# Fused attention and expert kernel: fewer, larger GpSimd operations between result scatters, and two small reorderings around the attention transposes

## The chip, the cores and the metric

The kernel runs on 1 core of one Trainium2 chip (trn2). The metric is the device time of one execution in microseconds (us). PE is TensorE, DVE is VectorE, ACT is ScalarE, POOL is GpSimd, and SP is the engine whose queue issues the plain DMAs. The kernel before takes 235.84 us, the median of three runs (235.73 to 238.3).

## The reference, cut to what matters

```python
x = L0_attn_x                                   # (4, 1024, 128) float32
xn = layernorm(x)
q, k = xn @ w_q, xn @ w_k                       # 64 columns each
attn = softmax(where(causal, q @ k.T * 64 ** -0.5, -inf))
attention = attn @ (xn @ w_v1 @ w_v2)
logits = xn @ w_router.T                        # 16 experts, top 1
s = sigmoid(logits) * one_hot(argmax(logits), 16)
gate, up = split((s * xn) @ gate_up_proj)       # 256 columns each, of the chosen expert
expert = (up * silu(gate)) @ down_proj
shared = silu(xn @ w_gate.T) * (xn @ w_up.T) @ w_down.T
out = x + attention + shared + expert
```

All of it is float32. The kernel splits each float32 operand of most products into a high and a low part and uses three products.

## The kernel before, in words

The 4096 tokens are 32 tiles of 128. They form 4 batches b = 0 to 3 of 8 tiles, each of two halves ("groups") of 4 tiles. Each engine has its own program, written out by hand; engines meet only at counting semaphores. An instruction waits at the head of its engine's queue until a semaphore has reached a value, and all behind it on that engine wait with it. Nothing is reordered by a planner. The program has these parts, with the times of the profiled execution:

- **Up to about 64 us**: layer norm, projections, router and shared expert. The router gives each token a slot in a table sorted by expert (48 tiles of 128 slots, 24 pairs of tiles).
- **Routing scatter, 59.6 to 111.9 us, on POOL (L454 to L459)**: 32 indirect DMAs write the token rows to their slots in DRAM (`scratch`), with a small weight subtraction (`weights_lo`, L428) after each. Beside it PE, ACT and DVE do the **attention of batches 0, 1 and half of 2** (`phase_c`).
- **Expert part, 114.8 to 203 us** (`phase_d`): for each of the pairs p = 0 to 23, SP loads 256 sorted rows (`xe`, two buffers), PE transposes them (`transpose_rows`), and three steps of PE, ACT and DVE make the result `y` (three buffers). POOL then scatters it to its tokens with two indirect DMAs (L505), 47 in all since the last pair has one tile.
- **The end, 203 to 233 us** (`phase_e`): attention of the other half of batch 2 and of batch 3 on PE, ACT and DVE. SP loads `y` back in 8 groups, POOL adds it to the residual (L513), and SP stores the result.

Around the change the names are these. In the expert part POOL runs a loop over the scatters t = 0 to 46 (pair p = t // 2). Ahead of each scatter it does small work: `keep_ids` (L461) copies the token numbers of pair p + 4 out of the `xe` buffer, `keep_scores` (L467) its scores, and `last_keys_hi` and `last_keys_lo` (L477, L480) split the keys of batch 3 in pieces of `K_PIECE` = 24 columns, 43 pieces of each kind for 1024 columns. The two key copies use only POOL's otherwise unneeded time; their result is first used by `scores` of batch 3 (L1237). SP issues the load of pair n + 2 into the buffer of pair n once PE has transposed pair n (`xet_done`) and POOL has kept both its ids and its scores (L354 to L357). POOL starts a pair's scatters once ACT has copied its result (`y_ready`, L494). PE's step p does gate and up of pair p, down of pair p - 2, the transposes of the hidden rows of pair p - 1 and the row transposes of pair p + 2 (L1370 to L1381); the registers that name the experts are loaded every second step (L1336).

In the attention, `scores(b, i)` computes the scores of tile i of batch b, DVE takes the row maximum (`row_max`), ACT the exponentials (`exp`, L1004, one per tile, counted in `exp_done`), PE transposes them block by block (`transposes(b, n)`, L1254), ACT copies the block (`keep_pt`) and PE multiplies it with the values (`weigh`). A block of `transposes` takes up to four tiles of one half and waits for the exponentials of all four before its first.

Of the kernel before, what the change touches and what calls it, by code (L numbers as in the profile page):

```python
# [30 lines left out]
GT = 4  # L31
# [6 lines left out]
def build(nc, x, w_small, w_gate_up, w_down, scratch, y_rows, out):  # L38
    B, S, EMB = x.shape
    NT = B * S // P  # L40
    NG = NT // GT
    BT = S // P
# [5 lines left out]
    NP = NS // 2  # L48
# [15 lines left out]
    with ExitStack() as ctx:  # L64
# [8 lines left out]
        def sb(name, shape, dt=F32):  # L73
            t = nc.alloc_sbuf_tensor_at(name, shape, dt, offset=top[0])
            top[0] += size(shape, dt)
            return t
# [55 lines left out]
        k_raw = sb("k_raw", [P, S])  # L132
        k_hi, k_lo = sb("k_hi", [P, S], F32R), sb("k_lo", [P, S], F32R)
# [39 lines left out]
        def sem(name, n=None):  # L173
            if n is None:
                return ctx.enter_context(nc.semaphore(name))
            return [ctx.enter_context(nc.semaphore(f"{name}{i}")) for i in range(n)]
# [27 lines left out]
        k_hi_ready, k_lo_ready, k_hi_pieces = sem("k_hi_ready"), sem("k_lo_ready"), sem("k_hi_pieces")  # L204
        s_done, max_ready, exp_done = sem("s_done"), sem("max_ready"), sem("exp_done")
# [29 lines left out]
        def flat(ap):  # L235
            return ap.rearrange("p a b -> p (a b)")
# [43 lines left out]
        def used(p):  # L280

            return 1 if isinstance(p, int) and p == NP - 1 else 2
# [94 lines left out]
        def _(pool):  # L377
# [83 lines left out]
            def keep_ids(p):  # L461

                q = p % 2
                pool.wait_ge(xe_loaded[q], 8 * (p - q) + 16)
                pool.tensor_copy(ids[:, 2 * p:2 * p + 2], xe[q][:, :, ID].bitcast(U32)).then_inc(ids_kept, 1)
# [5 lines left out]
                    pool.wait_ge(eh_ready, p - NY + 1)  # L471
                pool.tensor_copy(slot_score[:, p % NY, :], xe[q][:, :, SCORE]).then_inc(scores_kept, 1)

            def k_piece(n):
                return slice(n * K_PIECE, min((n + 1) * K_PIECE, S))

            def last_keys_hi(n):  # L477
                pool.tensor_copy(k_hi[:, k_piece(n)], k_raw[:, k_piece(n)]).then_inc(k_hi_pieces, 1)

            def last_keys_lo(n):  # L480
                cols = k_piece(n)
                pool.wait_ge(k_hi_pieces, n + 1)
                last = pool.tensor_tensor(k_lo[:, cols], k_raw[:, cols], k_hi[:, cols].bitcast(F32), ALU.subtract)
                if cols.start < S // 2 <= cols.stop or cols.stop == S:
                    last.then_inc(k_lo_ready, 1)
# [6 lines left out]
            for p in range(NP):  # L492
                pool.wait_ge(ids_kept, p + 1)
                pool.wait_ge(y_ready, p + 1)  # L494
                for t in range(2 * p, 2 * p + used(p)):
                    if t and p + AHEAD - 1 + t % 2 < NP:
                        if t % 2:
                            keep_scores(p + AHEAD)
                        else:
                            keep_ids(p + AHEAD - 1)  # L500
                    if t and (t - 1) * K_PIECE < S:
                        last_keys_hi(t - 1)
                    if t > 1 and (t - 2) * K_PIECE < S:
                        last_keys_lo(t - 2)
                    pool.indirect_dma_start(y_rows, bass.IndirectOffsetOnAxis(ap=ids[:, t:t + 1], axis=0),  # L505
                                            y[p % NY][:, t % 2, :], None, bounds_check=NT * P - 1,
                                            oob_is_err=False).then_inc(y_sent[p % NY], 16)

            for g in RETURN_ORDER:
                t = slice(g * GT, (g + 1) * GT)  # L510
# [6 lines left out]
        def _(dve):  # L517
# [62 lines left out]
            def add_shared(g):  # L580
                b, u = g // 2, g % 2
                dve.wait_ge(ffn_done, FIRST + g + 1)
                r = flat(res[:, bass.ds(g * GT, GT), :])
                dve.tensor_tensor(r, acc[u][:, :], r, ALU.add).then_inc(shared_added[u], 1)
# [222 lines left out]
            def first_half(b, first):  # L807
                if first:
                    for i in range(BT - 2):
                        row_max(b, i)  # L810
                        if i == 1:
                            add_shared(NG - 3)
                        if i == 4:
                            add_shared(NG - 2)
                            add_shared(NG - 1)
                row_max(b, BT - 2)
                row_max(b, BT - 1)
                if not first:
                    add_attention(b - 1, 1)
                if b == 1:  # L820
                    name_experts()
# [277 lines left out]
        def _(pe):  # L1099
# [154 lines left out]
            def transposes(b, n):  # L1254
                kb, c0 = block_of(n)
                g = 0 if n < GT else 1
                pe.wait_ge(exp_done, FIRST + b * BT + (g + 1) * GT)
                pe.wait_ge(pt_ready, FIRST + b * STEPS + max(n - 1, 0))
                if b == B - 2 and n == GT:
                    pe.wait_ge(xel_ready, NP)  # L1260
                if b == B - 2 and n == GT + 1:
                    pe.wait_ge(eht_ready, NP)
                for r in range(c0 // P, GT):
                    last = pe.transpose(mid[n % 2][:, r * P:(r + 1) * P],  # L1264
                                        prob[g * GT + r][:, kb * P:(kb + 1) * P], identf[:, :])
                last.then_inc(pt_done, 1)
# [20 lines left out]
            def first_half(b, first):  # L1287
                if first:
                    down(NG - 2)
                    for i in range(GT + 1):  # L1290
                        scores(b, i)
                    down(NG - 1)
                    pe.wait_ge(ranks_used, 1)
                    transposes(b, 0)
                else:
                    transposes(b, 0)
                    scores(b, BT - 1)
                if first:
                    scores(b, GT + 1)
                for n in range(GT):  # L1300
                    if first and n < 2:
                        scores(b, GT + n + 2)
                    if first and n == GT - 1:
                        weigh(b, n)
                        transposes(b, n + 1)
                        continue
                    if b == B - 2 and n == GT - 2:
                        pe.wait_ge(exp_done, FIRST + b * BT + BT - 1)
                        transpose_rows(0, 0)
                    if not (b == B - 2 and n == GT - 1):  # L1310
                        transposes(b, n + 1)
                    weigh(b, n)
                    if b == B - 2 and n == GT - 2:
                        pe.wait_ge(pt_ready, FIRST + b * STEPS + n + 1)
                        transpose_rows(1, 1)
# [89 lines left out]
CODE = 4  # L1405
NY = 3
AHEAD = 4
K_PIECE = 24
RETURN_ORDER = (0, 1, 2, 3, 4, 6, 7, 5)
FLY = 4  # L1410
FIRST = 1
# [36 lines left out]
```

## Time and profile before

| | |
|---|---|
| median of 3 runs | 235.84 us |
| profiled execution, its own time | 234.89 us |
| its span | 233.2 us |
| PE busy | 212.0 us, 91% |
| POOL busy | 158.1 us, 68% |
| POOL from the first result scatter to the end of the last | 127.69 to 207.21 us |
| TensorE clock granted | full throughout (1.00) |

The times in a profile line count from the start of the span. A timeline line has the start, the duration, the engine, the line of the kernel, the operation with the tensors it writes and reads, and how often it is repeated back to back; a bracket at the end tells how long the engine was idle before it and what released it ("issue" is a wait for nothing that the profile can name). Small operations on one engine overlap a little, so the distance from start to start is what counts.

### The profile page before, as it was taken

To read this page: it belongs to the slowest core of one execution; us is meant where nothing else is said; L and a number is where in the kernel's file an instruction comes from. 1 tells how busy PE (TensorE), PEld (TensorE's weight loads), DVE (VectorE), ACT (ScalarE), POOL (GpSimd) and SP (SyncE) were. 2 spreads that over 40 slices of the span, in tenths; PEclk is the share of its full clock that TensorE was granted. 3 is DMA by queue.
4 is the path that set the end of the run, shared out by engine and by line. 5 is a ranking of instruction groups with operands and counts; after the bars stand their busy time and mean duration, and the time that the engine had idled before them with its cause. 6 is when DMAs were issued, how large, how long until landed. Compare 5 with 4: busy or idle time off the path is not lost.

```text
span 233.2 us, 5014 instructions
## 1 busy us (share of the span) xinstructions
PE 212.0 (91%) x1415; PEld 182.3 (78%) x1417; DVE 146.2 (63%) x352; ACT 128.6 (55%) x305; POOL 158.1 (68%) x308
## 2 busy tenths in 40 slices
PE   4999999999997699899989999799989998899994
PEld 4978888897785598698767887677767786788794
DVE  3889679788764579879846657365456545304512
ACT  2377777877374556666764543344334424645741
POOL 3475956900788888888111989788988989845910
PEclk9999999999999999999999999999999999999999
DMA  6999999970181117215521122222231220009931
GB/s 132 337 381 300 274 208 200 155 291 3 40 210 45 35 49 179 82 37 135 133 67 42 56 80 54 80 70 65 79 87 52 77 78 10 0 6 285 297 90 46
DMA packets 30021, 28.27 MB, mean 121 GB/s; under 512 B 2579, under 2 KB 27162, under 8 KB 29360
## 3 DMA queue, kind: packets, MB, share of 16 engines
q1 hardware_dynamic: 27472, 23.77, 40.6%
q0 software_dynamic: 2528, 4.24, 5.9%
q8 instruction: 11, 0.18, 0.3%
q14 instruction: 10, 0.08, 0.1%
HBM read 14.28 MB, written 10.50 MB: 106 GB/s over the span
## 4 chain that ended last, share of the span: by engine, by line
PE 57%; POOL 21%; issue 8%; DMA 6%; DVE 3%; ACT 1%; SPq 1%; POOLq 0%; ACTq 0%
POOL scratch L457 14%; PE big L1103 7%; PE acc L1365 7%; PE big L1104 6%; PE big L1105 6%; POOL wel L431 5%; DMA xe<-scratch 5%; PE acc L1283 4%; PE acc L1163 4%; PE mid L1354 3%; PE mid L1264 3%; PE mid L1230 3%; PE mid L1113 2%; PE big L1283 2%; PE mid L1133 2%
## 5 line engine op out<-in xcount | busy, mean ns | idle before, releaser
L505 POOL DMA_INDIRECT y_rows<-y,ids x47 | 47.0, 1000 | 13.1 <-issue 8.2
L457 POOL DMA_INDIRECT scratch<-rows,slot x32 | 33.7, 1054 | 17.8 <-DVE slot L729 12.7
L1283 PE MATMUL acc<-vr_all,pt 128*128 128x128 f32 x246 | 35.9, 280 | 2.8 <-ACT pt L1016 2.1
L859 DVE COPY eht<-mid 128x512 f32<-128x512 f32 (+1 forms) x24 | 16.3, 681 | 33.5 <-PE mid L1354 22.9
L1283 PEld LDWEIGHTS acc<-vr_all,pt 128*128 128x128 f32 x246 | 31.6, 191 | 4.9 <-ACT pt L1016 2.3
L779 DVE TENSOR_REDUCE negmax<-big 128x1 f32<-128x128 f32 (+7 forms) x32 | 23.9, 754 | 18.1 <-PE big L1251 17.5
L1075 ACT COPY y<-acc 128x256 f32<-128x256 f32 (+1 forms) x24 | 8.8, 368 | 43.9 <-PE acc L1365 39.0
L1016 ACT COPY pt<-mid 128x512 f32<-128x512 f32 (+3 forms) x48 | 22.8, 475 | 17.0 <-PE mid L1264 14.9
L1004 ACT ACTIVATE prob<-big,negmax 128x128 f32<-128x128 f32 (+7 forms) x32 | 23.8, 743 | 14.1 <-DVE negmax L779 8.8
L1365 PEld LDWEIGHTS acc<-wed,eht 128*128 128x128 f32 x188 | 24.4, 191 | 3.8 <-issue 2.1
L1365 PE MATMUL acc<-wed,eht 128*128 x188 | 25.1, 276 | 1.3 <-DVE eht L859 1.3
L1103 PE MATMUL big<-weh,xeh 128*128 x47 | 20.7, 440 | 4.4 <-issue 3.8
L1264 PE MATMUL mid<-identf,prob 128*128 128x128 f32 x144 | 23.6, 274 | 0.7 <-ACT prob L1004 0.7
L865 DVE SCALAR_TENSOR_TENSOR eh<-esg,slot_score,big 128x256 f32<-128x256 f32 x47 | 20.5, 478 | 1.8 <-ACT esg L1082 1.3
L1082 ACT ACTIVATE esg<-big,slot_score 128x256 f32<-128x256 f32 x47 | 19.9, 478 | 1.2 <-PE big L1105 1.2
L1248 PE MATMUL big<-k_hi,q_hl 128*128 128x512 f32 (+3 forms) x48 | 18.6, 388 | 1.9 <-ACT prob L1004 1.6
L1251 PE MATMUL big<-k_lo,q_hl 128*128 128x512 f32 (+3 forms) x48 | 18.6, 393 | 0.0
L441 POOL TENSOR_SCALAR rows<-res,ln,ln 128x128 f32<-128x128 f32 x20 | 18.2, 918 | 0.5
L1105 PE MATMUL big<-weh,xel 128*128 x47 | 18.5, 393 | 0.0
L1104 PE MATMUL big<-wel,xeh 128*128 x47 | 18.4, 392 | 0.0
L1264 PEld LDWEIGHTS mid<-identf,prob 128*128 128x128 f32 x144 | 17.3, 142 | 1.4 <-ACT prob L1004 1.1
L393 POOL TENSOR_TENSOR ln<-ln,minus_half 128x4 f32<-128x4 f32 x8 | 8.9, 1115 | 10.1 <-DVE ln L557 10.1
(141 smaller groups left out, 473.5 us busy)
## 6 DMA issues: line engine op xcount, KB each, us to landing
we_raw<-w_gate_up SPq DMA_DIRECT2D x4, 1024.0 KB, 10.4
scratch<-blank SPq DMA_DIRECT2D x1, 3120.0 KB, 27.8
xe<-scratch SPq DMA_DIRECT2D x24, 130.0 KB
q_raw<-qk_all SPq DMA_DIRECT2D x8, 256.0 KB
k_raw<-qk_all SPq DMA_DIRECT2D x8, 256.0 KB
wed<-w_down SPq DMA_DIRECT2D x1, 2048.0 KB, 32.0
expert_out<-y_rows SPq DMA_DIRECT2D x8, 256.0 KB, 4.7
out<-res SPq DMA_DIRECT2D x7, 256.0 KB, 3.7
```

The costliest lines, as they stand in the source:

```text
L457: pool.indirect_dma_start(scratch, bass.IndirectOffsetOnAxis(ap=slot[:, t:t + 1], axis=0), rows[:, t, :], None).then_inc(row_sent[t % FLY] ...
L505: pool.indirect_dma_start(y_rows, bass.IndirectOffsetOnAxis(ap=ids[:, t:t + 1], axis=0), y[p % NY][:, t % 2, :], None, bounds_check=NT * P ...
L779: dve.tensor_reduce(negmax[:, i:i + 1], buf[:, at:at + (i + 1) * P], AX.X, ALU.max, negate=True).then_inc(max_ready, 1)
L865: last = dve.scalar_tensor_tensor(out=eh[q][:, v, :], in0=esg[q][:, v, :], scalar=slot_score[:, m, v:v + 1], in1=big[q][:, v * GC + FE:(v ...
L1004: act.activation(prob[i][:, 0:(i + 1) * P], buf[:, at:at + (i + 1) * P], ACT.Exp, bias=negmax[:, i:i + 1], accum_out=den[:, i:i + 1]).then ...
L1016: act.copy(pt[n % 2][:, c0:GC], mid[n % 2][:, c0:GC]).then_inc(pt_ready, 1)
L1103: pe.matmul(dst, wh, mh, start=True, stop=False)
L1104: pe.matmul(dst, wh, ml, start=False, stop=False)
L1105: return pe.matmul(dst, wl, mh, start=False, stop=True)
L1264: last = pe.transpose(mid[n % 2][:, r * P:(r + 1) * P], prob[g * GT + r][:, kb * P:(kb + 1) * P], identf[:, :])
L1283: last = pe.matmul(weighed(b, g, r), pt[n % 2][:, cols], v, start=kb == 0 and (r == 0 or own_bank), stop=True, skip_group_check=True)
L1365: last = pe.matmul(acc[q][:, v * P:(v + 1) * P], eht[q][:, v, c, :], flat(wed[:, bass.ds(e[v], 1), c * P:(c + 1) * P]), start=c == 0, stop ...
```

## The change

- The low parts of batch 3's keys are made in pieces of 48 columns, one per pair, in place of 24 columns ahead of each scatter. The high parts stay at 24 columns. `last_keys_lo` waits for the two high pieces that it covers.
- `keep_ids` moves from the even scatter of the next pair to the odd scatter, right behind `keep_scores`.
- In batch 0, `scores(0, 5)` comes ahead of the first block of transposes.
- `transposes` waits for the exponentials of each tile just before that tile's transpose, in place of all four before the first.
- DVE adds the shared expert's last group one row maximum later.

```diff
+            def last_keys_hi(half):
+                cols = slice(half * K_PIECE // 2, min((half + 1) * K_PIECE // 2, S))
+                if cols.start < S:
+                    pool.tensor_copy(k_hi[:, cols], k_raw[:, cols]).then_inc(k_hi_pieces, 1)
             def last_keys_lo(n):
-                pool.wait_ge(k_hi_pieces, n + 1)
+                cols = slice(n * K_PIECE, min((n + 1) * K_PIECE, S))
+                pool.wait_ge(k_hi_pieces, min(2 * n + 2, -(-2 * S // K_PIECE)))
...
                 for t in range(2 * p, 2 * p + used(p)):
-                    if t and p + AHEAD - 1 + t % 2 < NP:
-                        if t % 2:
+                    if t % 2:
+                        if p + AHEAD < NP:
                             keep_scores(p + AHEAD)
-                        else:
-                            keep_ids(p + AHEAD - 1)
-                    if t and (t - 1) * K_PIECE < S:
-                        last_keys_hi(t - 1)
-                    if t > 1 and (t - 2) * K_PIECE < S:
-                        last_keys_lo(t - 2)
+                            keep_ids(p + AHEAD)
+                        last_keys_hi(2 * p)
+                    elif p:
+                        last_keys_hi(2 * p - 1)
+                        if 1 < p and (p - 2) * K_PIECE < S:
+                            last_keys_lo(p - 2)
...
-                        if i == 4:
+                        if i == GT:
                             add_shared(NG - 2)
+                        if i == GT + 1:
                             add_shared(NG - 1)
...
-                pe.wait_ge(exp_done, FIRST + b * BT + (g + 1) * GT)
                 pe.wait_ge(pt_ready, FIRST + b * STEPS + max(n - 1, 0))
...
                 for r in range(c0 // P, GT):
+                    pe.wait_ge(exp_done, FIRST + b * BT + g * GT + r + 1)
...
                     pe.wait_ge(ranks_used, 1)
-                    transposes(b, 0)
-                else:
-                    transposes(b, 0)
+                    scores(b, GT + 1)
+                transposes(b, 0)
+                if not first:
                     scores(b, BT - 1)
-                if first:
-                    scores(b, GT + 1)
...
-K_PIECE = 24
+K_PIECE = 48
```

On POOL, in the expert part, two pairs of scatters before:

```order
L465 COPY ids<-xe_92 128x2
L478 CAST k_hi<-k_raw 128x24
L483 TENSOR_TENSOR k_lo<-k_raw,k_hi 128x24
L505 DMA y_rows<-y_145,ids 4096x128
L472 COPY slot_score<-xe_95 128x2
L478 CAST k_hi<-k_raw 128x24
L483 TENSOR_TENSOR k_lo<-k_raw,k_hi 128x24
L505 DMA y_rows<-y_145,ids 4096x128
```

and the same place in the changed kernel:

```order
L477 CAST k_hi<-k_raw 128x24
L482 TENSOR_TENSOR k_lo<-k_raw,k_hi 128x48
L504 DMA y_rows<-y_146,ids 4096x128
L472 COPY slot_score<-xe_92 128x2
L465 COPY ids<-xe_92 128x2
L477 CAST k_hi<-k_raw 128x24
L504 DMA y_rows<-y_146,ids 4096x128
```

Ahead of the even scatter there was an ids copy, a high and a low piece and ahead of the odd one a scores copy and the same; now the even one has a high and a wider low piece, and the odd one has both copies and a high piece. That is five operations per pair in place of six.

On PE, after the down product of the last group in batch 0 (`prob_123` to `prob_127` are the exponentials of tiles 0 to 3), before:

```order
L1264 MATMUL mid<-identf,prob_123 128x128 [waits pt_ready,exp_done,ranks_used]
L1264 MATMUL mid<-identf,prob_124 128x128
L1264 MATMUL mid<-identf,prob_125 128x128
L1264 MATMUL mid<-identf,prob_127 128x128
L1248 MATMUL big<-k_hi,q_hl 128x512 [waits exp_done]
L1251 MATMUL big<-k_lo,q_hl 128x512
```

and now:

```order
L1248 MATMUL big<-k_hi,q_hl 128x512 [waits exp_done,ranks_used]
L1251 MATMUL big<-k_lo,q_hl 128x512
L1248 MATMUL big<-k_hi,q_hl 128x256
L1250 MATMUL big<-causal,identb 128x128
L1251 MATMUL big<-k_lo,q_hl 128x256
L1264 MATMUL mid<-identf,prob_123 128x128 [waits exp_done,pt_ready]
L1264 MATMUL mid<-identf,prob_124 128x128 [waits exp_done]
L1264 MATMUL mid<-identf,prob_125 128x128 [waits exp_done]
L1264 MATMUL mid<-identf,prob_127 128x128 [waits exp_done]
```

The scores of tile 5 stand ahead of the block, and each transpose of a block carries a wait of its own. The second of these holds for all 48 blocks of the kernel (144 transposes, 96 waits more).

## Rows read from the trace of the kernel before

**Rows 1.** The page, part 2: busy tenths in 40 slices of 5.83 us.
```profile
PE   4999999999997699899989999799989998899994
...
POOL 3475956900788888888111989788988989845910
```
**Rows 2.** POOL's timeline: a full round from one scatter (t = 3) to the next.
```profile
132.60 1.00 POOL L505 DMA_INDIRECT y_rows<-y,ids  x1 [0.17 <-issue]
133.61 0.20 POOL L465 COPY ids<-xe 128x2 uint32<-128x2 uint32 x1
133.74 0.21 POOL L478 CAST k_hi<-k_raw 128x24 fp32r<-128x24 f32 x1
133.90 0.24 POOL L483 TENSOR_TENSOR k_lo<-k_raw,k_hi 128x24 fp32r<-128x24 f32 x1
134.31 1.01 POOL L505 DMA_INDIRECT y_rows<-y,ids  x1 [0.17 <-issue]
```
**Rows 3.** PE's timeline: starts of steps 3 and 4, last row transposes (end of step 21).
```profile
126.81 0.47 PE L1103 MATMUL big<-weh,xeh 128*128 x1
...
129.74 0.47 PE L1103 MATMUL big<-weh,xeh 128*128 x1
...
192.65 0.43 PE L1230 MATMUL mid<-identf,xe 128*128 128x128 f32 x2
```
**Rows 4.** Waits on PE, 119 to 203 us: us in total, times, longest.
```profile
PE big L1103 <- issue: 3.8, 9, 0.9
PE mid L1230 <- DMA xe<-scratch: 2.4, 4, 1.6
```
**Rows 5.** Waits of SP's queue over the whole span, same columns.
```profile
SPq L356 <- POOL ids L465: 25.9, 9, 3.2
```
**Rows 6.** POOL's timeline: places where it was late, and the last ids before a load.
```profile
142.14 0.48 POOL L472 COPY slot_score<-xe 128x2 f32<-128x2 f32 x1
...
151.73 0.18 POOL L465 COPY ids<-xe 128x2 uint32<-128x2 uint32 x1 [0.78 <-issue]
...
176.15 0.18 POOL L465 COPY ids<-xe 128x2 uint32<-128x2 uint32 x1 [0.43 <-issue]
...
188.18 0.20 POOL L472 COPY slot_score<-xe 128x2 f32<-128x2 f32 x1
...
189.91 0.18 POOL L465 COPY ids<-xe 128x2 uint32<-128x2 uint32 x1
```
**Rows 7.** ACT's timeline: the copy of pair 7's result.
```profile
151.23 0.37 ACT L1075 COPY y<-acc 128x256 f32<-128x256 f32 x1 [2.12 <-PE acc L1365]
```
**Rows 8.** Chain of waits: start, duration, what.
```profile
110.30 4.38 DMA scratch<-rows,slot
...
144.55 3.66 DMA xe<-scratch
```
**Rows 9.** Line L431: shortest/median/longest in ns, 64 columns each.
```profile
L431 POOL TENSOR_TENSOR wel<-we_raw,weh x32: 325/330/761, 61.3 to 111.6; 128x64 fp32r<-128x64 f32 x32
```
**Rows 10.** PE's timeline: first transposes of batch 3's second half.
```profile
220.64 0.66 PE L1264 MATMUL mid<-identf,prob 128*128 128x128 f32 x4 [0.34 <-ACT prob L1004]
```
**Rows 11.** Timelines of POOL (sums 2 to 6) and DVE (batch 3, first half).
```profile
213.59 6.22 POOL L513 TENSOR_TENSOR res<-res,expert_out 128x512 f32<-128x512 f32 x5 [0.77 <-DMA expert_out<-y_rows]
...
221.65 1.13 DVE L799 SCALAR_TENSOR_TENSOR res<-acc,rden,res 128x128 f32<-128x128 f32 x4 [0.83 <-PE acc L1283]
```
**Rows 12.** Timelines of POOL and DVE at the same moment of the routing scatter.
```profile
79.70 0.76 POOL L431 TENSOR_TENSOR wel<-we_raw,weh 128x64 fp32r<-128x64 f32 x1
...
79.59 0.69 DVE L701 TENSOR_TENSOR k_lo<-k_raw,k_hi 128x512 fp32r<-128x512 f32 x1
```
**Rows 13.** Line L1124, one wait per transpose: columns as in rows 9.
```profile
L1124 PE MATMUL acc<-identf,rows x32: 270/272/332, 9.0 to 47.7; 128*128 128x128 f32 x32
```
**Rows 14.** The page, part 5: attention transposes (count, busy us, mean ns).
```profile
L1264 PE MATMUL mid<-identf,prob 128*128 128x128 f32 x144 | 23.6, 274 | 0.7 <-ACT prob L1004 0.7
L1264 PEld LDWEIGHTS mid<-identf,prob 128*128 128x128 f32 x144 | 17.3, 142 | 1.4 <-ACT prob L1004 1.1
```

More of the change, by code:

```diff
@@ L472, in keep_scores @@
                 pool.tensor_copy(slot_score[:, p % NY, :], xe[q][:, :, SCORE]).then_inc(scores_kept, 1)
[L474 to L478, printed above, removed]
+            def last_keys_hi(half):
+                cols = slice(half * K_PIECE // 2, min((half + 1) * K_PIECE // 2, S))
+                if cols.start < S:
+                    pool.tensor_copy(k_hi[:, cols], k_raw[:, cols]).then_inc(k_hi_pieces, 1)
             def last_keys_lo(n):
-                cols = k_piece(n)
-                pool.wait_ge(k_hi_pieces, n + 1)
+                cols = slice(n * K_PIECE, min((n + 1) * K_PIECE, S))
+                pool.wait_ge(k_hi_pieces, min(2 * n + 2, -(-2 * S // K_PIECE)))
                 last = pool.tensor_tensor(k_lo[:, cols], k_raw[:, cols], k_hi[:, cols].bitcast(F32), ALU.subtract)
```

## The prediction

> **What bounds the kernel now.** I read the busy slices of the page first: PE and POOL are both nearly full from 115 to 207 us [rows 1], so the page alone doesn't tell which of them sets the pace of the expert part. POOL's timeline does. From one scatter to the next it takes 134.31 - 132.60 = 1.71 us [rows 2], 1.705 on average over such rounds, with no gap but the 0.17 us ahead of each scatter; a pair is two rounds, 3.41 us. PE's steps 3 and 4 start 129.74 - 126.81 = 2.93 us apart when their rows are there [rows 3]. But from the start of step 4 to the row transposes at the end of step 21 there are 192.65 - 129.74 = 62.9 us for 18 steps less a few tenths, about 3.5 a step. So PE could be half a microsecond per pair faster and is held: by rows that are not loaded, 2.4 us, and by short waits at the head of every second step, 3.8 us, which come mostly where the row transposes before them had to wait too [rows 4]. What holds the loads is seen in SP's waits: its load waits last for POOL's ids, 25.9 us [rows 5]. POOL is the bound of the expert part, and through the ids it paces PE.
>
> There is a second thing to see. POOL itself was late at two places: at 151.73 after 0.78 us idle, and at 176.15 after 0.43 [rows 6]. The first one's cause is the result of pair 7, whose copy ended at 151.23 + 0.37 = 151.60 [rows 7]. That result was late because PE stood until 148.2 for a load issued at 144.55 that took 3.66 us [rows 8], and that load had waited for POOL's ids. It is a loop: ids of pair n, load of n + 2, four PE steps, result of n + 2, scatter of n + 2. From the ids of pair 5 at 133.61 [rows 2] to that result it is 18.0 us, and POOL had 10 rounds of 1.705 = 17.05 us for it. The loop has next to no slack.
>
> After 203 us PE is nearly without a gap again, and the end follows PE. What makes PE leave the expert part earlier is worth its full size.
>
> **The change part by part.** I number the rounds by the scatter that ends them, t = 0 to 46.
>
> *Low pieces and ids, on POOL.* Start to start, a copy takes 133.74 - 133.61 = 0.13 us, a high piece followed by another operation 0.16 (I take 0.17), and the last operation its own duration and 0.17 us [rows 2]. A low piece of 24 columns takes 0.235 on average; one of 64 columns 0.33 [rows 9]. That is 0.095 for 40 columns, so 48 columns take 0.235 + 24 / 40 * 0.095 = 0.29. The ends are 0.235 (width free) and 0.33 (as for 64). The round before the even scatter becomes 1.01 + 0.17 + 0.29 + 0.17 = 1.64, the one before the odd scatter, with both copies and a high piece of 0.20, 1.01 + 0.13 + 0.13 + 0.20 + 0.17 = 1.64. Each was 1.705.
>
> *Where the ids come now.* The last load, of pair 23, needs the ids of pair 21. They came at 189.91 [rows 6], at the even scatter t = 36. They now stand behind the scores ahead of t = 35. Count to there: t = 3 was at 132.60 [rows 2]. It moves by a copy more at t = 1 (+0.13), a copy and a low piece less at t = 2 (-0.28) and one shorter round (-0.065), to 132.39. t = 4 to 35 are 32 rounds of 1.64, 184.87; the ids start 0.20 + 0.17 + 0.13 ahead of that scatter, at 184.37. That is 189.91 - 184.37 = 5.54 us earlier. It is made up of these terms:
> - 1.60, one place earlier: the scores before stood at 188.18 [rows 6], plus 0.13 for their copy, against 189.91;
> - 2.23, shorter rounds: 31 times 0.065 up to t = 34 (t = 35's own is in the first term, with the scores' place), and the 0.21 up to t = 3;
> - 1.42, the two waits for results, which cost rounds of 2.58 and 2.24 us in place of 1.705. They go because the loop now has 11 rounds of 1.64 = 18.04 us for the 18.0 that the slow load made it take. That is just enough, so the term's lower end is nothing;
> - 0.29 at 142.14, where a copy took 0.48 us in place of 0.20 [rows 6] for no reason that the trace shows. I leave that out, since it may come again.
>
> So the load of pair 23 is issued 5.25 us earlier. Is PE there in time? At 2.93 a step from 129.74 on, its step 21 would end at 182.5, 10.5 us before the 193.1 of the trace, so it stays ahead of the loads even if some short waits remain. SP also waits for PE's transposes of pair 21, at the end of step 19, which come some 4 us before the new ids. Nothing is queued behind the moved ids that would wait on them: they wait for a load that landed two pairs earlier.
>
> *Key pieces.* The last low piece moves from t = 44 to t = 46, new time near 201.5; the scores that need it run at 211.6 before and some 206 now. It costs nothing; without that cover the price would be two rounds, 3 us.
>
> *Transposes tile by tile.* At 220.64 PE waited 0.34 us for the last exponential of batch 3 [rows 10]. Three of the four transposes of that block, 0.11 us each, can now go first: 0.3 us, on the path. At the other blocks of the end no such wait stands. In batches 0 to 2 (up to 117 us) PE's gains, and those of moving the sixth scores and DVE's add, are worth nothing: the expert part starts when POOL's last routing scatter has landed, 110.30 + 4.38 us [rows 8], and PE waits for that load anyway. If that cover were gone, it would be PE's order that counts, some tenths either way.
>
> *The start of the expert part* can still move. In the routing scatter a weight subtraction of POOL takes 0.33 us, but 0.76 at 79.70, beside a DVE subtraction that reads two SBUF tensors [rows 9, 12]. DVE's work there shifts a little. Such collisions add up to 50.7 us from first to last scatter against 31 undisturbed rounds of 1.505 = 46.7, 4 us in all. I take no change, with a quarter of it, 1 us, as either end. The Trainium skill says why such a pair collides (SBUF — State Buffer, "Who interferes with whom": a VectorE instruction with two SBUF inputs contends with a GpSimd one that reads SBUF, and the second to issue blocks fully); this trace agrees with 0.76 against 0.33.
>
> *Sum*: 5.25 + 0.3 = 5.55 us. The profiled execution took 234.89 us (span 233.2), so 229.3; it lies 0.95 under the median, so the median goes from 235.84 to **230.3**. POOL's scatters end at about 203.0 in place of 207.21, 4.2 earlier. Its sixth sum (219.81 before) comes at 215.6, DVE's add that needs it at 221.65 - 5.55 = 216.1 [rows 11]: just in time, and PE doesn't wait for it.
>
> **The rivals.**
> - *The loop stays tight.* Slow loads like the one at 144.55 still stall POOL (1.42 stays), and the wide pieces cost as much as 64 columns, with 0.03 more on the odd rounds (16 * 0.04 + 16 * 0.03 = 1.1 us). For it: 18.04 against 18.0. Against: one place is gained for all loads, and the second stall needed only 17.4. 5.55 - 1.42 - 1.1 = 3.0, so 232.8.
> - *PE becomes the bound.* If the 3.8 us of short waits are PE's own (register loads), only the 2.4 for rows and 0.3 can be had [rows 4]: 2.7, so 233.1. For it: they follow the load of expert registers. Against: steps 4 and 10 load them too, and show no gap.
> - *The early ids don't start loads earlier* (the scores or SP hold them, so the change doesn't do what it says): 1.60 and 1.42 fall away, 2.5 stays, 233.3. Against: ids were last 9 times at that wait [rows 5], and the scores already stood one place earlier.
> - *Slower: the waits of single transposes expose weight loads.* A weight load of a transpose is 142 ns [rows 14] and lies beside the matmul before it. If an instruction that waits could not have its weights loaded ahead, each of the 42 waits added after 199 us costs 0.142, 6.0 us; the 54 added before 117 us 7.7, of which PE's waits up to there, some 5 us in all, cover all but 2.5. -5.25 + 6.0 + 2.5 = 3.3 slower, 239.1. It turns the sign from 0.11 us per wait on. Against: the 32 transposes of L1124 carry a wait each and take 272 ns, as the 274 of those without [rows 13, 14].
> - *Collisions move against it* by a microsecond: 231.3.
>
> **How the numbers follow.** Forecast 0.56, with its own range of 229.2 to 231.4 (low pieces 0.235 to 0.33, 0.8 either way, and tenths at the last load). The tight loop 0.14, PE the bound 0.08, ids without effect 0.04, the slower case 0.04, collisions against it 0.07, and in its favour 0.07 (229.3). Between 228.9 and 233.5 lie all but the slower case and the outer parts of the others, less than 2 in 10. Two per cent, about what a measurement of this kernel can tell from no change, is 4.7 us, 231.1. Faster than that: 0.45 of the forecast, the favourable collisions 0.06 and 0.01 of the rest, 0.52. Slower than 240.6 takes the slower case at a higher price per wait: 0.03. Within: 0.45.
>
> **What would show it.** In the profile after: rounds of POOL of 1.64 us, low pieces of 48 columns of 0.29 us; no idle time of half a microsecond ahead of a pair; the last row transposes near 187.4; SP's waits ended by ids still; transposes of 274 ns; scatters over by 203 us; four transposes no longer in one piece after the last exponential. The prediction is wrong if the first result scatter is not near 127.7, if PE's steps settle above POOL's 3.28 us per pair, or if the stretch from the last row transposes to the end, 40.6 us before, grows.

## The result and the profile after

The changed kernel takes 228.41 us in the median of four runs (227.92 to 229.38), the kernel before 236.33 in four runs beside it; the ratio is 0.9656, with an interval of 0.9589 to 0.9724. It is faster by 3.4%. The forecast was 230.3 with a range down to 228.9, so the kernel came out 0.5 us under the range. All ratios of this document, and their intervals, leave out the runs that lie more than 1.5% above the fastest of the same kernel.

The profiled execution took 229.38 us with a span of 227.2. The other three runs had spans of 226.4 to 227.0: the profile shows the longest of the four.

The page, part 2 (slices of 5.68 us), answers to [rows 1], with the row of the TensorE clock that was granted (tenths of full speed) beneath:

```profile
PE   4899999999999799999939999989989998899994
...
POOL 3465874930488888888711489989898989861960
PEclk9999999999999999999997999999999999999999
```

From slice 24 to 35 POOL is about as full as PE; before, that stretch was 13 slices long, and they were longer. In one slice the granted clock was not full, and in the slice ahead of it PE was busy for only 3 tenths.

POOL's timeline answers to [rows 2] with a pair of rounds, and to the last of [rows 6] with the ids of pair 21, at 184.78 in place of 189.91:

```profile
177.18 1.00 POOL L504 DMA_INDIRECT y_rows<-y,ids  x1 [0.17 <-issue]
178.18 0.20 POOL L472 COPY slot_score<-xe 128x2 f32<-128x2 f32 x1
178.30 0.20 POOL L465 COPY ids<-xe 128x2 uint32<-128x2 uint32 x1
178.42 0.21 POOL L477 CAST k_hi<-k_raw 128x24 fp32r<-128x24 f32 x1
178.80 0.98 POOL L504 DMA_INDIRECT y_rows<-y,ids  x1 [0.16 <-issue]
179.79 0.21 POOL L477 CAST k_hi<-k_raw 128x24 fp32r<-128x24 f32 x1
179.96 0.28 POOL L482 TENSOR_TENSOR k_lo<-k_raw,k_hi 128x48 fp32r<-128x48 f32 x1
180.40 1.01 POOL L504 DMA_INDIRECT y_rows<-y,ids  x1 [0.16 <-issue]
...
184.78 0.19 POOL L465 COPY ids<-xe 128x2 uint32<-128x2 uint32 x1
```

From scatter to scatter it takes 1.62 and 1.60 us. The low piece of 48 columns takes (the row of its line: count, shortest/median/longest in ns)

```profile
L482 POOL TENSOR_TENSOR k_lo<-k_raw,k_hi x22: 230/284/307, 133.9 to 201.5; 128x48 fp32r<-128x48 f32 x21, 128x16 fp32r<-128x16 f32 x1
```

Waits of PE from 119 to 197 us, and of SP's queue over the span, answer to [rows 4, 5]:

```profile
PE big L1103 <- issue: 3.5, 8, 1.0
PE acc L1363 <- DVE eht L859: 0.7, 2, 0.4
PE mid L1230 <- DMA xe<-scratch: 0.2, 1, 0.2
```
```profile
SPq L356 <- POOL ids L465: 47.4, 18, 4.5
```

PE's waits for rows are gone from this trace (in the second trace of the changed kernel one of 1.3 us stands), its short waits at the heads of steps are not, and the loads still go out on POOL's ids. The last row transposes stand at 187.55, in place of 192.65 [rows 3]. At the start of the expert part PE's timeline has this:

```profile
116.56 0.41 PE L1230 MATMUL big<-identf,xe 128*128 128x128 f32 x2 [3.11 <-DMA xe<-scratch]
...
118.57 0.63 PE L1103 MATMUL big<-weh,xeh 128*128 x1 [0.44 <-issue]
119.00 0.63 PE L1104 MATMUL big<-wel,xeh 128*128 x1
119.43 0.63 PE L1105 MATMUL big<-weh,xel 128*128 x1
```

The same place before the change:

```profile
117.14 0.41 PE L1230 MATMUL big<-identf,xe 128*128 128x128 f32 x2 [0.77 <-DMA xe<-scratch]
...
119.57 0.40 PE L1104 MATMUL big<-wel,xeh 128*128 x1
119.80 0.39 PE L1105 MATMUL big<-weh,xel 128*128 x1
```

PE waited 3.11 us for the first rows, 0.77 before the change. Then its matmuls start 0.43 us apart; before, at full clock, they started 0.23 apart.

**The span in stretches.** I cut it at six marks: first and last routing scatter, first row transposes on PE, first result scatter, last row transposes, and the transposes with which PE is out of the expert part (203.12 before, 197.90 now). All in us, from start to start; "landing" runs from the last routing scatter to the first row transposes.

| kernel | routing scatters | landing | to first result | expert loop | exit | tail | clock |
|---|---|---|---|---|---|---|---|
| before | 50.67 | 6.84 | 10.55 | 64.96 | 10.47 | 30.08 | 1.000 |
| changed | 51.50 | 5.18 | 11.56 | 59.43 | 10.35 | 29.30 | 0.992 |

### The profile page after: what moved, and what is told of

Its sections match the earlier page's. It is cut to its first block, busy times and chain, and to the rows that moved or that the text cites. A ratio compares the mean times of both kernels' runs of the same rounds, so it can differ in the third digit from the quotient of the medians.

```text
span 227.2 us, 4994 instructions
## 1 busy us (share of the span) xinstructions
PE 209.2 (92%) x1415; PEld 182.6 (80%) x1417; DVE 145.3 (64%) x352; ACT 128.7 (57%) x305; POOL 155.8 (69%) x287
## 4 chain that ended last, share of the span: by engine, by line
PE 58%; POOL 23%; issue 7%; DMA 7%; DVE 3%; ACT 1%; SPq 0%; POOLq 0%
POOL scratch L457 14%; PE acc L1363 8%; PE big L1103 8%; PE big L1105 7%; PE big L1104 6%; POOL wel L431 6%; PE acc L1283 5%; PE acc L1163 4%; PE mid L1352 4%; DMA ws_raw<-w_small 3%; PE mid L1264 3%; DMA xe<-scratch 2%; PE mid L1230 2%; PE big L1283 2%; PE mid L1133 2%
## 5 line engine op out<-in xcount | busy, mean ns | idle before, releaser
L1283 PE MATMUL acc<-vr_all,pt 128*128 128x128 f32 x246 | 35.3, 278 | 1.6 <-ACT pt L1016 1.6
L1103 PE MATMUL big<-weh,xeh 128*128 x47 | 21.3, 454 | 3.5 <-issue 3.5
L1105 PE MATMUL big<-weh,xel 128*128 x47 | 19.0, 404 | 0.0
L1104 PE MATMUL big<-wel,xeh 128*128 x47 | 19.0, 403 | 0.0
```

The lines of the kernel that those rows point to most:

```text
L1103: pe.matmul(dst, wh, mh, start=True, stop=False)
L1104: pe.matmul(dst, wh, ml, start=False, stop=False)
L1105: return pe.matmul(dst, wl, mh, start=False, stop=True)
L1283: last = pe.matmul(weighed(b, g, r), pt[n % 2][:, cols], v, start=kb == 0 and (r == 0 or own_bank), stop=True, skip_group_check=True)
```

## The experiments

Each was timed in turn with the kernel before, whose median in the three groups of runs was 235.28, 234.75 and 235.27 us. The stretches of all of them stand in one table behind the texts.

**Both kernels again.** No edit.

> The changed kernel once more, unaltered, to see how much of the 7.9 us between the medians is the kernel and how much is the spread of the runs. Theory A (the traces are right: the span fell by 6.0 us, and my placing of the median above the profiled run was wrong): the difference of the medians comes out at 6 to 7 us, about 229 against 235.5. Rival (something that no profile shows adds to the gain): 7.9 us again or more, 228.4 against 236.3. In the trace TensorE's clock dips again right after the idle time ahead of the first sorted rows.

> The kernel before, unaltered, for a second trace. The one that I predicted from had the full clock throughout, and 17 further runs of that kernel have a mean granted clock of 0.985 to 0.999 and 232.95 to 236.33 us. If its trace was untypical: this one shows a dip of the clock somewhere after 56 us, the first sorted rows before 117.14, and the stretch from first result scatter to last row transposes longer than 64.96 us (the run with the attention part alone had 65.64). If it was typical: the same within 0.3 us in each stretch.

The changed kernel took 228.35 us (six runs), ratio 0.9664 [0.9617, 0.971]. A second trace of the kernel before (one run, 236.22) has another picture than the first. POOL's two late places, of [rows 6], are larger, 1.21 and 0.51 us in place of 0.78 and 0.43:

```profile
156.14 0.18 POOL L465 COPY ids<-xe 128x2 uint32<-128x2 uint32 x1 [1.21 <-issue]
...
177.27 0.18 POOL L465 COPY ids<-xe 128x2 uint32<-128x2 uint32 x1 [0.51 <-issue]
```

and PE waited 2.16 us for the first rows, with the same slow stretch behind it. These are PE's row and two windows (length, busy us of PE, PEld, DVE, ACT, POOL, granted clock, DMA share, GB/s):

```profile
116.32 0.41 PE L1230 MATMUL big<-identf,xe 128*128 128x128 f32 x2 [2.16 <-DMA xe<-scratch]
```
```profile
118.00:120.00 2.00, 1.58 (x4) 1.31 (x5) 1.61 (x6) 1.42 (x2) 0.34 (x3) 0.50 0.51 116
120.00:122.00 2.00, 2.00 (x9) 1.55 (x8) 0.00 (x0) 0.71 (x2) 0.15 (x1) 0.75 0.00 0
```

So the trace on which the forecast was built is the quicker of the two, and almost all of that lies in the loop, 0.8 us. It also has 1.2 less between the first rows and the first result, but its first rows came 1.1 later: from first routing scatter to first result the two take 68.06 and 68.30 us.

The times of the two kernels, sorted by mean granted clock, can be compared as well. Beside the changed kernel, the kernel before has a median of 233.55 us in its 3 runs at a clock of 0.998 or more and 235.40 in the 14 others; the changed kernel has 226.15 in 2 and 228.58 in 4. With the clock alike they are 7.4 and 6.8 us apart.

**The change in halves: POOL's part, and the attention part** (scores first, waits by tile, DVE's add). Each is the kernel before with the hunks of the diff that are POOL's, or all the others.

> The kernel before with the GpSimd part of the change alone (48-column low pieces, ids behind the scores), attention as before. If the expert part gives its gain by itself: from first to last row transposes 5.5 us less, TensorE idle only 0.8 us ahead of the first rows, so no clock dip, first result scatter at 127.7. Gain 5.5 us, 230.3 against 235.8; with the 1.0 us of the clock not lost, even as fast as the full change to within 0.6 us. Rival (the attention part is needed for the gain): 2 us or more slower than the full change.

> The kernel before with the attention part of the change alone (scores of tile 5 first, transposes waiting tile by tile, the later shared add). My account: TensorE reaches the first sorted rows some 3 us early, idles there and loses about 1.0 us to the lower clock; the rows land 0.6 us earlier; the expert part keeps GpSimd's old pace; the end gains 0.3 to 0.8 us. Net between 0.5 us faster and 0.5 slower, 235.3 to 236.3. Rival (tile-by-tile waits are worth something in every block): 1.5 us faster or more, 234.3.

POOL's part: 229.35 us (226.36 to 232.35, six runs; the trace is the fastest one's), 0.9726 [0.9682, 0.977]. The attention part: 234.75, 0.998 [0.9947, 1.0012]. Against the medians beside them these are 5.9 and 0.5 us. The gain is POOL's.

**POOL's part in halves.** The ids alone, with pieces as before:

```diff
-                    if t and p + AHEAD - 1 + t % 2 < NP:
-                        if t % 2:
-                            keep_scores(p + AHEAD)
-                        else:
-                            keep_ids(p + AHEAD - 1)
+                    if t % 2 and p + AHEAD < NP:
+                        keep_scores(p + AHEAD)
+                        keep_ids(p + AHEAD)
```

and the pieces alone: POOL's part as changed, with `keep_ids(p + AHEAD - 1)` left ahead of the even scatter.

> The kernel before with the ids copied behind the scores, low pieces as before (24 columns, six operations per pair). My terms: one place earlier 1.6 us and the two waits for results 1.4 us gone, so 3.0 us faster, 232.3 against 235.3; rounds stay at 1.70 us; no idle time of half a microsecond ahead of a pair. Rival (the shorter rounds are all of it): nothing, 235.3. Second rival (the early ids are most of it, since with a lead TensorE runs at its own pace): 4 us or more, 231.

> The kernel before with low pieces of 48 columns once per pair, ids at the even scatter as before (five operations per pair). My term: rounds of 1.64 us, 2.2 us over the stretch, the waits for results stay or grow, since the ring has 10 rounds of 1.64 = 16.4 us for a way of some 17.5: then GpSimd waits for results and the gain is 0 to 1 us, 234.3 to 235.3. Rival (rounds are what counts): 2.2 us, 233.1.

Ids alone: 231.63 us, 0.9866 [0.9808, 0.9923]; the loop takes 62.24 and POOL is never late in it. Pieces alone: 234.11, 0.9944 [0.9896, 0.9992]; the loop takes 62.84, and POOL is late in five places, by 1.92 us in all. The longest:

```profile
173.76 0.19 POOL L465 COPY ids<-xe 128x2 uint32<-128x2 uint32 x1 [0.75 <-issue]
```

Shorter rounds do not take the late places away; the earlier ids do. In the loops of these traces, against the second trace of before (65.75), the two are worth 3.5 and 2.9 us, and 6.3 together (59.44). That they add up so is not shown: the trace of the pieces alone is of one of the three fastest of its twelve runs (232.55). Against the medians beside them the ids alone gain 3.1 us, the pieces alone 0.6, within the 0 to 1 that was put down for the case that POOL then waits for results, and both together 5.9.

**The attention part in halves.** Scores first (with DVE's add), and the waits by tile:

```diff
                 for r in range(c0 // P, GT):
+                    pe.wait_ge(exp_done, FIRST + b * BT + g * GT + r + 1)
```

> The kernel before with the scores of tile 5 ahead of the first transposes and the later shared add, nothing else. If this is what brings TensorE early to the first sorted rows: an idle time of about 3 us there, the clock dip behind it, rows landing 0.6 us earlier, and the time of the attention part alone, 234.8 (-0.5). If the tile-by-tile waits do it: TensorE idle 0.8 us there as before and 235.3.

> The kernel before with the waits of the transposes tile by tile, nothing else. My term: 0.3 us at the last exponential, in the trace the distance from the first transposes after the expert part to the last ones 0.3 us shorter (25.7 against 26.0), each transpose still 274 ns; 0.3 us of 235, below what the runs can tell. Rival (the 0.85 us by which the end is shorter with the attention part, 29.3 against 30.1, are all these waits'): 0.8 us shorter.

Scores first: 235.27 us, 1.0027 [0.9988, 1.0065]. Waits by tile: 235.07, 1.0013 [0.9975, 1.0051]. No median shows either. The stretch to the first result holds a dip of the clock in both traces, behind waits of PE of 2.06 and 2.13 us. In the tail of the second, PE's transposes at the last exponential, with the wait of 0.34 in [rows 10], are

```profile
220.44 0.84 PE L1264 MATMUL mid<-identf,prob 128*128 128x128 f32 x4
```

Three have gone ahead and the fourth follows, 0.84 us from first start to last end in place of 0.66, with no idle time ahead. From the block ahead of it to the second one behind it takes 223.01 - 219.88 = 3.13 us, and 223.03 - 219.57 = 3.46 before. The whole tail of that trace is 0.9 us shorter, though, as its rival had it; of the rest more below.

**PE kept busy ahead of the first rows.** The changed kernel, and the kernel before with 16 in place of 20. The added transposes fill a buffer that nobody reads:

```diff
-                        pe.wait_ge(exp_done, FIRST + b * BT + BT - 1)
+                        pe.wait_ge(exp_done, FIRST + b * BT + BT)
+                        for _ in range(20):
+                            pe.transpose(big[1][:, 0:P], identf[:, :], identf[:, :])
                         transpose_rows(0, 0)
```

> The changed kernel with 20 idle transposes (0.11 us each, result unused) on TensorE between its last attention work and the first sorted rows, where it stood 3.1 us. If the idle time is what lowered the clock: granted clock 1.00 throughout, the first gate and up products 0.23 us apart in place of 0.43, first result scatter 1.0 us earlier (127.1), and the whole 0.7 to 1.0 us faster than the changed kernel, 227.6. Rival (GpSimd or the loads set the end whatever TensorE does there): the clock is full and the time is the same, 228.4; or the dip comes all the same, at the same place.

> The kernel before with 16 idle transposes on TensorE ahead of the first sorted rows, so that neither this nor the changed kernel with 20 of them loses clock there. Theory A (clock and change are independent, the change is worth its 6.3 us in the expert part and 0.3 to 0.8 at the end): 1.1 us under the kernel before where that one dips, 233.5, and 6.6 to 7.1 us above the changed kernel kept busy (226.9). Rival (the dip is paid by the changed kernel alone): no gain here, 234.8, so 8 us apart.

The changed kernel so took 226.85 us (226.44 to 227.93, six runs), 0.9653 [0.9623, 0.9682]; its clock was 0.999 or 1.000 in every run. Beside it on the same chip the changed kernel itself ran in 225.93 and 226.37 with a clock of 1.000 and 0.998, and in 228.22 to 229.38 with 0.985 to 0.992. The two intervals overlap, and the two fastest runs of the changed kernel are faster than all of these. So it is not shown that the added work makes the kernel faster; the medians (1.5 us) point that way, and what it shows is that the clock then stays full. In the trace:

```profile
115.80 0.42 PE L1230 MATMUL big<-identf,xe 128*128 128x128 f32 x2
...
117.82 0.50 PE L1103 MATMUL big<-weh,xeh 128*128 x1 [0.40 <-issue]
118.16 0.40 PE L1104 MATMUL big<-wel,xeh 128*128 x1
118.39 0.39 PE L1105 MATMUL big<-weh,xel 128*128 x1
```

There is no idle time ahead of the rows, the same matmuls start 0.23 to 0.34 us apart, and the stretch to the first result is 10.45. In the kernel before it made that stretch 10.42, but it gave 234.3, 0.998 [0.9944, 1.0016]. There PE waits 0.44 us for one exponential more, the added transposes take from 115.61 to 117.41, and the first rows come later (landing 7.59). 1.0 us of that lateness, against the second trace of before, is PE's already ahead of the added work, in a trace with a dip of the clock at 78 to 84 us. Ten of its twelve runs have a clock of 0.998 or more, with a median of 234.13; the kernel before itself has 233.79 in 12 such runs beside it. Nothing was won.

**Larger pieces.** With PE kept busy, `K_PIECE` is 128, then 512.

> The changed kernel kept busy, with low pieces of 128 columns and high ones of 64 (16 high and 8 low pieces in place of 43 and 22), so the key work is over by scatter 18 and later rounds are some 1.3 us. If GpSimd still bounds the expert part: the stretch from first result scatter to last row transposes falls from 59.4 to 57 us or less, 224.5. If TensorE's own step has become the bound (3.19 us per step in the trace of the changed kernel against 3.24 us for GpSimd's pair): less than 0.5 us, 226.5.

> The same with low pieces of 512 columns and high ones of 256: all key work in the first six rounds. Rounds 1 to 6 get 0.5 to 1.5 us longer, all later ones are short. If only the total of GpSimd's work counts: as fast as pieces of 128 or faster. If the scatters' start matters, since every id waits behind them: TensorE waits for rows at steps 4 to 8 and it is 1 us slower than pieces of 128, 227.5.

They gave 234.74 us, 0.9972 [0.9931, 1.0013], and 236.14, 1.0064 [1.002, 1.0108]. The times put down for them all missed; only that 512 columns are slower than 128 (1.4 us) had been one of the outcomes. Fewer and larger operations lose all that 48 columns had gained. Of the 8.2 us between the spans of 48 and 128 columns (225.0 and 233.2) 3.5 lie in the loop, 2.5 at the exit and 1.4 in the tail; the other 0.9 lie ahead of the first result, where the two kernels are the same. At the exit the clock was down, 0.59 from 202 to 204 us, behind 2 us in which PE was busy for 0.06; but the five runs with a clock of 0.998 or more have a median of 234.64, so the clock is not what costs most. The pieces end early, at 157 and 138 us. After that POOL has only copies and scatters and catches up with the results. POOL's waits from 126 to 205 us, first with 48 columns, then with 128 (both with PE kept busy; the first result, 4.7 us, is in both):

```profile
POOL y_rows L504 <- issue: 7.1, 42, 0.3
POOL y_rows L504 <- ACT y L1075: 5.3, 5, 4.7
```
```profile
POOL y_rows L504 <- ACT y L1075: 13.6, 8, 4.7
POOL y_rows L504 <- issue: 9.4, 38, 1.3
POOL y_rows L504 <- POOL ids L465: 0.2, 1, 0.2
```

A loop that waits for PE should run at PE's pace, 2.93 us a step in [rows 3]. It doesn't: late in the run two pairs take 181.51 - 174.47 = 7.04 us, 3.52 each, more than POOL's 3.23 in the changed kernel. What I see is that from 173 us on every second result is copied late. With 128 columns, PE, then ACT and DVE:

```profile
178.11 1.05 PE L1365 MATMUL acc<-wed,eht 128*128 x8
179.00 0.60 PE L1354 MATMUL mid<-identf,eh 128*128 128x128 f32 x4
```
```profile
180.31 0.37 ACT L1075 COPY y<-acc 128x256 f32<-128x256 f32 x1 [3.30 <-PE acc L1365]
```
```profile
180.37 0.69 DVE L859 COPY eht<-mid 128x512 f32<-128x512 f32 x1 [2.39 <-PE mid L1354]
```

The down product is over at 179.16 by its rows and the copy starts at 180.31; with 48 columns the copy follows after 0.1 us. What ACT and DVE both wait for there no row shows. It stays open. There is a second loss, seen in these rows of ACT and POOL from two results earlier:

```profile
173.27 0.37 ACT L1075 COPY y<-acc 128x256 f32<-128x256 f32 x1 [1.42 <-PE acc L1365]
```
```profile
174.47 0.97 POOL L504 DMA_INDIRECT y_rows<-y,ids  x1 [1.96 <-ACT y L1075]
```

The copy ends at 173.64 and the scatter starts 0.83 us later. In the kernel before, POOL waited for a result too, but had the ids' copy to do first, and that started 0.13 us after the result's copy had ended (151.60, 151.73). No run tested what a small operation kept ahead of the scatter would give back.

All stretches, columns as in the table above:

| kernel | routing scatters | landing | to first result | expert loop | exit | tail |
|---|---|---|---|---|---|---|
| before, second trace | 50.83 | 5.73 | 11.74 | 65.75 | 10.47 | 30.12 |
| changed, second trace | 51.51 | 5.25 | 11.33 | 59.52 | 10.22 | 29.23 |
| POOL's part | 50.06 | 6.06 | 10.42 | 59.44 | 10.17 | 29.60 |
| attention part | 51.48 | 5.25 | 11.72 | 65.64 | 10.34 | 29.28 |
| ids alone | 50.71 | 5.77 | 11.64 | 62.24 | 10.48 | 29.53 |
| pieces alone | 50.93 | 5.56 | 11.29 | 62.84 | 10.47 | 30.23 |
| scores first alone | 50.82 | 5.64 | 11.84 | 65.55 | 10.47 | 30.17 |
| waits by tile alone | 50.92 | 5.70 | 11.55 | 65.58 | 10.47 | 29.23 |
| changed, PE busy | 51.50 | 4.76 | 10.45 | 59.36 | 10.14 | 29.25 |
| before, PE busy | 50.16 | 7.59 | 10.42 | 64.52 | 10.33 | 30.22 |
| 128 columns, PE busy | 50.89 | 6.26 | 10.42 | 62.83 | 12.63 | 30.62 |
| 512 columns, PE busy | 50.83 | 6.26 | 10.42 | 65.26 | 13.12 | 30.14 |

## Why the prediction was off, step by step

**What held.** POOL was the bound and paced PE through the ids: earlier ids alone give 3.1 us and take POOL's late places away, both halves of POOL's part shorten the loop in the traces, and the attention part doesn't. One thing was overlooked: in the trace before, the wait of SP's queue ends 9 times with the ids (25.9 us) and 9 times with the scores (12.8 us). That the ids alone, moved, shorten the loop shows that they count. The ids of pair 21 came at 184.78 (forecast 184.37) and the last row transposes at 187.55 (187.4). The 48-column piece takes 284 ns (290), the scatters were over at 202.9 (203.0), and the transposes kept their 274 ns:

```profile
L1264 PE MATMUL mid<-identf,prob 128*128 128x128 f32 x144 | 23.9, 274 | 0.0
```

so the slower rival fell, also by itself in the waits by tile alone. DVE's add in the tail was not "just in time". By POOL's row (six sums from 211.92 on in 7.41 us) the sixth sum ended near 216.9 and not at 215.6, and the add waited 1.87 us for it. PE did not wait for the add, so it cost nothing:

```profile
216.92 1.13 DVE L798 SCALAR_TENSOR_TENSOR res<-acc,rden,res 128x128 f32<-128x128 f32 x4 [1.87 <-POOL res L512]
```

Profile against profile the sum looks exact: 234.89 became 229.38, with 229.3 forecast. Part of that is luck. The spans differ by 6.0 us: 5.5 in the loop (5.25 forecast), 0.8 in the tail (0.3) and 0.1 at the exit (nothing), less 0.4 by which the first result came later (nothing). The missing 0.5 is time outside the spans.

**What failed: the last step, from the profile to the median.** It read "it lies 0.95 under the median, so the median goes from 235.84 to 230.3". That carries the offset of one execution of before over to the changed kernel, whose profile then lay 0.97 us above its median and not 0.95 under it. These 1.9 us are the whole way from 230.3 to 228.41. The offset is no constant: the profiles of the two second traces lie 1.5 above the median of the group beside it (before) and 0.1 under its own (changed).

With that the sum itself was too small. From median to median the change is worth 235.28 - 228.35 = 6.9 us beside each other on one chip, and 7.9 in the four runs of each, where 5.55 was forecast. The clock is no explanation for that, since the two kernels are 6.8 and 7.4 us apart with the clock alike. In the profiles the two errors hid each other: the measured profile of the changed kernel was a slow one of its kind, and the gain larger than forecast.

**Terms that were mis-sized:**
- The loop: 5.25 forecast; 64.96 - 59.43 = 5.5 measured against the trace of the forecast, 65.75 - 59.52 = 6.2 between the second traces. The ids were put at 1.60 for the place and 1.42 for the late places, 3.0. Alone they gave 3.5 in the loop against the second trace, and 0.3 of the 0.5 more is that its late places are 1.7 us; by the medians they gave 3.1. Shorter rounds were put at 2.23. Alone they gave 2.9 in the loop of a fast trace and 0.6 by the medians. With the ids they are shorter than forecast: from pair 5's even scatter (144.80) to pair 20's (193.35) the changed kernel has 30 rounds in 48.55 us, 1.618 each, not 1.64; 31 times 0.087 and the 0.21 up to t = 3 are 2.9 in place of 2.23.
- The reason given for the late places was half wrong. I had them go because 11 rounds of 1.64 just cover the slow load's way. With rounds as before and early ids they go (ids alone), with short rounds and late ids they stay (pieces alone). It is the place of the ids, the eleventh round, that gives the loop its slack; shorter rounds take from it.
- The tail: 0.3 forecast, 30.12 - 29.23 = 0.9 measured. The waits by tile give 0.33 at the last exponential, as forecast. The other half microsecond comes at the start of the tail. It is there in the run with the waits by tile alone, whose rival had put all of the 0.8 down to these waits; but the ids alone, without them, have it too (29.53). Two copies `pt` of ACT start 1.53 us apart with the change (198.54, 200.07) and 2.02 without it (203.76, 205.78), in both traces of before; the idle time ahead of the second is 0.95 and 1.44, though PE's transposes for it are over. The parts don't single out a cause: the tail is 29.2 to 29.6 with POOL's part, the ids, the attention part or the waits by tile, and 30.2 with the pieces or the scores first. It stays open.
- The start of the expert part was put at nothing, with 1 us either way. In the trace of the attention part the routing scatters take 0.65 us longer than in the second trace of before, as the rival of collisions had it, and the landing 0.5 less; together that is nearly nothing. Both traces of the changed kernel and the one with PE busy have these 51.5 us as well, but the two with larger pieces, which are the same kernel up to there, have 50.89 and 50.83. So that the attention part does it isn't shown. But ahead of the first result there was a term that I did not have at all, the clock.

The rivals: with a loop of 59.4 us neither "the loop stays tight" nor "early ids don't start loads earlier" holds, and PE was not the bound at 3.23 us a pair, although it kept 3.5 us of short waits. The last of the prediction's signs of being wrong, a longer way from the last row transposes to the end, did not show: 39.65 us by the table, 40.55 before.

## What to carry to other kernels

One profile of before is one execution. Before a sum from a profile is laid on a median, ask which of its terms vary from run to run (late places, the granted clock, the first landing), and take the offset between profile and median as part of the range, not as a constant. In a loop over several engines, move what starts the next transfer forward first, and shorten rounds second: here the first paid 3.1 us alone, the second 0.6 alone, and both together 5.9. Fewer and larger pieces of side work make the sum of an engine's work smaller, and still the kernel can lose by them: here 48 columns in every pair beat 128 and 512 that end early. Why is only known in part, so try both.

## What the runs showed of the hardware

- The clock. In all eight traces in which PE stood still for 1.99 to 3.19 us ahead of the first rows, its granted clock fell around the end of that wait, to between 0.50 and 0.53 in a window of 2 us (0.50 is the lower level, 1.2 GHz), and was full again by 124 us. Where it stood 0.72 or 0.77 us, or was kept busy, the clock stayed full there. With the dip the stretch up to the first result takes 0.7 to 1.4 us more (11.29 to 11.84 against 10.42 to 10.55). It is no constant of the kernel: of six runs of the changed kernel two had a mean clock of 0.998 or more, and took 225.93 and 226.37 us.
- A dip can cost nothing. The trace of POOL's part had its dip at 78 to 82 us, while POOL's routing scatters set the end, and has the shortest span of all traces, 224.9 us. The kernel before with PE busy had one there too, at 78 to 84, behind 2 us in which PE was busy for 0.99. In the second trace of before that is 0.89 us, with no dip behind it. These two traces with an early dip also have the shortest routing scatters, 50.06 and 50.16 us; whether the one comes from the other isn't shown.
- A POOL that waits for a result and has the scatter itself next starts it 0.83 or 0.84 us after the end of the result's copy (with 128 columns at 162.93, 173.27, 180.31, 187.38, 194.30 and 200.43). Where a small copy is next, as in the kernel before at 151.73, that starts after 0.13 us, and a POOL that is behind starts its scatter after 0.16 to 0.17 us of idle time.
